# A transformer block on one core: causal runs with their masked key tiles between full ones, keys stored once and read in halves, and the last block's expert rows returned to tokens by products with ones

## The reference, cut to what matters

```python
x = layernorm(x + attention(x))            # causal, 16 heads of 8, rotary q and k
h = x + msa(layernorm(x) * ln1_w + ln1_b)  # 16 heads of 8, every key seen, no mask
h = h + moe(layernorm(h) * ln2_w + ln2_b)
out = layernorm(x + h)

def moe(x):                                # 8 experts, hidden size 512
    e = argmax(x @ gate_w + gate_b)        # one expert for each token, the first of equals
    return gelu(x @ w1[e]) @ w2[e]
```

## Time and profile before

| | us |
|---|---|
| median of three runs | 893.57 |
| the profiled execution | 894.7 |
| its span, first to last instruction | 893.0 |
| TensorE busy | 809.2 (91%) |
| ScalarE busy | 775.7 (87%) |
| VectorE busy | 328.5 (37%) |
| GpSimd busy | 228.5 (26%) |
| mean granted TensorE clock | 0.959 |
| exp, L922, 832 instructions | 736.0 busy |
| first scores start | 33.31 |
| last run's sums taken by VectorE (L1312) | 815.87 |

### The profile page before, as it was taken

How to read it: one execution, slowest core, us unless ns; L and a number is a source line. 1 busy time by engine, 2 the same in 40 slices (tenths; PEclk the granted TensorE clock), 3 DMA queues, 4 the chain that set the end, 5 groups by cost and what they waited for, 6 DMA issues and landing times.

```text
span 893.0 us, 24266 instructions
## 1 busy us (share of the span) xinstructions
PE 809.2 (91%) x9940; PEld 369.5 (41%) x9952; DVE 328.5 (37%) x948; ACT 775.7 (87%) x906; POOL 228.5 (26%) x367
## 2 busy tenths in 40 slices
PE   8689999999999998999999999999999999996271
PEld 4244444444443443444344444444444444443240
DVE  5434525312430014320042433255332363334763
ACT  3579889999999998999999999999999899994440
POOL 5542211111110010000003343323334141443382
PEclk9799999999999999999999999999999999998575
DMA  8977220202110431810201000301000010001001
GB/s 273 269 210 224 96 49 2 95 2 49 49 48 1 108 84 40 244 50 3 48 2 32 1 3 3 78 8 37 3 3 19 14 43 3 1 3 31 30 14 41
DMA packets 34644, 51.60 MB, mean 58 GB/s; under 512 B 4064, under 2 KB 15072, under 8 KB 34528
## 3 DMA queue, kind: packets, MB, share of 16 engines
q1 hardware_dynamic: 32992, 46.30, 18.2%
q0 software_dynamic: 1536, 3.67, 1.3%
HBM read 29.12 MB, written 20.84 MB: 56 GB/s over the span
## 4 chain that ended last, share of the span: by engine, by line
PE 76%; DVE 8%; ACT 4%; issue 4%; DMA 2%; SPq 2%; POOL 2%; POOLq 1%; another core or an unknown queue 1%; DVEq 0%; ACTq 0%
PE ps L488 72%; ACT probs L922 3%; PE ps L493 3%; PE ps L787 1%; POOLq L1070 1%; DMA query_rows<-q_scratch 1%; POOL parts L1077 1%; DVE ln_newton L1156 1%; DMA q_scratch<-parts 1%; DVE q_rotated L1312 1%; DVE ln_newton L1155 1%; DVE z_rows L1176 1%; DVE ln_stats L1161 0%; DVE ln_newton L1154 0%
## 5 line engine op out<-in xcount | busy, mean ns | idle before, releaser
L922 ACT ACTIVATE probs<-ps 128x1024 f32<-128x1024 f32 (+3 forms) x832 | 736.0, 1017 | 41.5 <-PE ps L488 35.1
L488 PE MATMUL ps<-probs,values 128*9 128x256 f32 (+1 forms) x6528 | 426.3, 374 | 4.7 <-DVE q_rotated L1312 3.1
L488 PE MATMUL ps<-query_rows,key_rows 32*128 32x512 f32 (+3 forms) x1664 | 282.5, 485 | 17.5 <-ACT probs L922 10.2
L488 PEld LDWEIGHTS ps<-probs,values 128*9 128x9 f32 x6528 | 143.3, 90 | 182.5 <-issue 94.4
L488 PEld LDWEIGHTS ps<-query_rows,key_rows 32*128 32x128 f32 x1664 | 117.3, 183 | 183.5 <-issue 93.1
L1043 POOL TENSOR_SCALAR_AFFINE_SELECT probs<-probs 128x256 f32<-128x256 f32 x128 | 53.0, 420 | 234.4 <-ACT probs L922 231.5
L1090 POOL COPY parts<-early_late 128x512 f32 x63 | 44.5, 744 | 124.6 <-PE ps L488 124.6
L1048 POOL DMA_INDIRECT z_sorted<-z_rows,slot_numbers x16 | 15.8, 988 | 218.3 <-DVE slot_numbers L1447 208.8
L1312 DVE COPY q_rotated<-ps 128x512 f32<-128x512 f32 x30 | 20.7, 690 | 124.7 <-PE ps L488 124.6
L1077 POOL COPY parts<-parts 128x512 f32 x72 | 44.9, 663 | 29.3 <-PE ps L488 28.8
L1324 DVE RECIPROCAL recip<-ps 128x16 f32<-128x16 f32 x32 | 8.2, 256 | 70.5 <-PE ps L493 65.1
(11 more groups left out here) (184 smaller groups left out, 586.4 us busy)
## 6 DMA issues: line engine op xcount, KB each, us to landing
k_scratch<-parts SPq DMA_DIRECT2D x16, 512.0 KB, 3.9
q_scratch<-parts SPq DMA_DIRECT2D x16, 512.0 KB, 5.5
query_rows<-q_scratch SPq DMA_DIRECT2D x32, 256.0 KB, 5.3
key_rows<-k_scratch SPq DMA_DIRECT2D x20, 256.0 KB, 4.6
key_rows<-k_scratch SPq DMA_DIRECT2D x16, 192.0 KB, 4.5
parts<-in_w SPq DMA_DIRECT2D x1, 2048.0 KB, 8.9
early_late<-in_w SPq DMA_DIRECT2D x8, 256.0 KB, 8.0
early_late<-z_sorted SPq DMA_DIRECT2D x4, 384.0 KB, 3.1
```

The lines of the kernel that those rows point to most:

```text
L488: return nc.tensor.matmul(out, l, r, start=start, stop=stop, skip_group_check=True)
L922: nc.scalar.activation(Pr[:, t % KEPT, 2 * p:2 * p + 2, lo:BLK], score_banks(t, p)[:, :, lo:BLK], ACT.Exp, bias=-SHIFT[r["a"]], scale=SCAL ...
```

## The change

Its parts, in the order of the program:

1. **Loads.** Weights, block mask and identity move from SP's queue to ScalarE's queue; VectorE rotates block 0 before it waits for the identity.
2. **Keys stored once.** `k_scratch` loses a dimension: a block of keys is written by one DMA of 512 KB in place of two, and read by eight DMAs of 16 partitions in place of four of 32 (the same bytes). Queries are as before.
3. **First rows.** Of block 0, group 0's key and query rows are read first, with semaphores of their own; the other groups' rows follow.
4. **Order of key tiles.** The masked tiles of a causal run are dealt between full ones.
5. **Inverse root.** One cubic step (four small operations) takes the place of two Newton steps (six) in the layer norm; the same in `rows_to_h`, where the last `due` becomes one step earlier than `z_turn`.
6. **Routing.** Two reductions and three operations on all four tiles take the place of `max`, `max_index` and the rest.
7. **Gathers** of blocks 0 and 1 are paced at steps 4, 6, 8 and 10.
8. **Last block.** `up` of round 2 stands before `turn` of round 0; `up` of round 0 waits for the first turned tile alone. The store and the four gathers go away: a row of slot numbers is made by a product with ones, VectorE makes for each round a 128 by 512 matrix of ones and zeros, and TensorE sums `ones` times results over the six rounds (`m_sum`, four products each) in one bank, which VectorE adds.

```diff
-RDMA = 16 * HG
+RDMA, KDMA = 16 * HG, 16 * HG * NP
+ORDER = (
+    (0, 1, 2, 3),
+    (0, 1, 2, 3, 6, 4, 7, 5),
+    (0, 1, 2, 3, 4, 5, 11, 6, 10, 7, 9, 8),
+    (0, 1, 2, 3, 4, 5, 6, 7, 8, 15, 9, 14, 10, 13, 11, 12),
+)
-AT_END = side_order(*(range(first, first + 6 * ROUNDS, 6) for first in (30, 38, 43)))
+AT_END, TAKEN_AT_END = (side_order((30, 36, third, 48, 54, 60), range(38, 74, 6), range(43, 79, 6)) for third in (37, 42))
 ...
         def keys_out(a, b):
             sp.wait_ge(A[a]["k_split"], b + 1)
-            for i in range(NP):
-                sp.dma_start(k_scratch[a - 1, i, ...], k3[:, b]).then_inc(k_out[b], 16)
+            sp.dma_start(k_scratch[a - 1, ...], k3[:, b]).then_inc(k_out[b], 16)
+        def key_rows_in(a, g0, g1, t0, t1, done):
+            src = k_scratch[a - 1].rearrange("j d (g f) t -> f (j d) g t", f=HG)
+            each = ROWS // NP
+            for n in range(HG * NP):
+                sp.dma_start(kaf[n * each:(n + 1) * each, g0:g1, t0:t1], src[n // NP, :, g0:g1, t0:t1]).then_inc(done, 16)
+        def first_rows():
+            sp.wait_ge(k_out[0], 16)
+            key_rows_in(1, 0, 1, 0, BLK, k_first)
+            sp.wait_ge(q_out[0], 32)
+            query_rows_in(1, 0, 0, 1, q_first)
+            key_rows_in(1, 1, G, 0, BLK, k_rows[0])
+            query_rows_in(1, 0, 1, G, q_rows[0])
+        def places_in():
+            sp.wait_ge(evac_done, len(RUNS))
+            sp.dma_start(given_places, places_d).then_inc(ld_n, 16)
 ...
         def keys_there(r):
+            if r["n"] == 0:
+                pe.wait_ge(k_first, KDMA)
+                pe.wait_ge(q_first, RDMA)
+                return
 ...
-                side_free(b, k, ("sorted", 1))
+                side_free(b, k, ("sorted", 4 * r * TS // BLK))
+        def m_dest_rows():
+            pe.wait_ge(m_diag, 1)
+            mm(ps[:, 0, :], onesf[:, :], att[...]).then_inc(m_row, 1)
+        def m_sum(r):
+            pe.wait_ge(m_taken, taken(b, "down", r))
+            pe.wait_ge(m_at, r + 1)
+            for i in range(TB):
+                last = mm(ps[:, 1, i * P:(i + 1) * P], ones_at[r].bitcast(F32)[:, i * P:(i + 1) * P], yS[:, r, :],
+                          r == i == 0, r == ROUNDS - 1)
+        m_dest_rows()
         for k, (_, name, r) in enumerate(AT_END):
+            if name == "down" and r:
+                m_sum(r - 1)
             side_op[name](b, k, r)
+        m_sum(ROUNDS - 1)
 ...
         # scalar queue: the loads of wa, blk, ident first; wo ... kc after the first Exp
+                if r >= 2:
+                    act.wait_ge(m_side, issued(b, "turn", r - 2))   # before xg[r % 2] is written
         # gpsimd
+                if b == NB - 1:
+                    return
-                        pace(first_step(2, b + 2) + 1 + i)
+                        pace(first_step(2, b + 2) + 4 + 2 * i)
         # vector
+            def root_start(y, h, c, var, v):
+                ts(c, var, CUBIC, CUBIC * EPS, ALU.mult, ALU.add)
+                ts(h, var, -0.5, -0.5 * EPS, ALU.mult, ALU.add)
+                link(ts(y.bitcast(I32), v.bitcast(I32), -0.5, 1597463007.0, ALU.mult, ALU.add))
+            def cubic(y, c, t, u):
+                link(tt(t, y, y, ALU.mult))
+                link(tt(t, t, c, ALU.mult))
+                link(stt(out=u, in0=t, scalar=-1.25 / CUBIC, in1=t, op0=ALU.add, op1=ALU.mult))
+                link(stt(out=y, in0=u, scalar=1.875, in1=y, op0=ALU.add, op1=ALU.mult))
-                rsqrt(y, v, h, t, 1)
+                root_start(y, h, c, mv[:, :, 1], v)
+                cubic(y, c, t, u)
                 between()
-                newton(y, h, t, 2)
+                newton(y, h, t, 1)
-                due(13)
+                due(PREP_AT[b][0] - 1)
 ...  # route
-                max, max_index, copy, four is_equal
+                link(nc.vector.tensor_reduce(mx, lg[:, :, :], AX.X, ALU.max))
+                link(tt(oh, lg, mx, ALU.is_equal))
+                link(tt(lg, oh, first_wins, ALU.mult))
+                link(nc.vector.tensor_reduce(mx, lg[:, :, :], AX.X, ALU.max))
+                link(tt(oh, lg, mx, ALU.is_equal))
+            def dest_diag():
+                for i in range(TB):
+                    ins = ts(att[:, i, :], ident[:, :], destf[:, i:i + 1], None, ALU.mult)
+                ins.then_inc(m_diag, 1)
+            def ones_of(r):
+                dve.wait_ge(ld_n, 16)
+                dve.wait_ge(m_row, 1)
+                ts(ones_at[r], ps[:, 0, :], place_of[:, r:r + 1], None, ALU.is_equal).then_inc(m_at, 1)
 ...  # end of the program on VectorE
             route(b)
+            dest_diag()
             add_experts(b - 1)
             finish(b - 1)
-            experts(b, AT_END, at_once)
-            for i in range(TB):
-                dve.wait_ge(m_tile[i], 16)
-                link(tt(row, row, yback[:, i, :], ALU.add))
-                last = nc.vector.bn_stats(st[:, i, :], row)
-            normalize(xb, xb).then_inc(m_out, 1)
+            experts(b, TAKEN_AT_END, at_once)      # ones_of(r) behind the gelu argument of round r
+            dve.wait_ge(m_summed, 1)
+            link(tt(xb, xb, ps[:, 1, :], ALU.add))
+            layernorm(xb, xb).then_inc(m_out, 1)
```

More of the change, by code:

```diff
@@ L38 @@
 THETA = 10000.0
+CUBIC = float(np.sqrt(3.0 / 8.0))
 P = 128
@@ L320, in build @@
             sem(n) for n in ("a2_z", "a2_zT", "a2_hT", "k_blockdiag_set", "low_mm", "low_taken"))
+        ld_n = sem("ld_places")
+        m_diag, m_row, m_at, m_summed = (sem(f"m_{n}") for n in ("dest_diag", "dest_rows", "ones_at", "y_summed"))
         m_z, m_zT, m_h, m_g, m_oh, m_rank, m_dest, m_owner = (
             sem(f"m_{n}") for n in ("z", "zT", "h", "g", "oh", "rank", "dest", "owner"))
-        m_tile = [sem(f"m_y_back_tile{i}") for i in range(TB)]
         m_w1_last = sem("m_w1_staged_last")
@@ L341, in build @@
         kaf, qaf = KAv.bitcast(F32), QAv.bitcast(F32)
+        ones_at = [(KAv[:, 3, r * BLK:(r + 1) * BLK] if r < 4 else KAv[:, r - 3, S - BLK:S]) for r in range(ROUNDS)]
+        given_places = Pr[:, KEPT - 1].rearrange("p h t -> p (h t)")[:, 0:SORTED + ROUNDS]
+        places, place_of = given_places[:, 0:SORTED], given_places[:, SORTED:SORTED + ROUNDS]
         values_of = {1: V, 2: V2}
@@ L349, in run_step @@
         def run_step(r, n):
-            causal, kt = r["a"] == 1, r["k0"] + n
+            causal = r["a"] == 1
+            order = ORDER[r["qb"]] if causal else range(r["k0"], r["k1"])
+            kt = order[n]
             cut = causal and kt >= r["qb"] * TB
-            done = sum(TB for q in RUNS[:r["n"]] if q["a"] == 1)
+            done = r["n"] * TB + sum(k >= r["qb"] * TB for k in order[:n])
             return dict(r=r, t=r["t0"] + n, kt=kt, lo=(kt % TB) * P if cut else 0,
-                        cut=2 * (done + kt % TB) + 1 if cut else None, start=n == 0, stop=kt == r["k1"] - 1)
+                        cut=2 * done + 1 if cut else None, start=n == 0, stop=n == len(order) - 1)
         block = ctx.enter_context(nc.Block())
@@ L402, in query_rows @@
                 sp.wait_ge(q_out[b], 32 * a)
[L403 to L409 removed]
+                query_rows_in(a, b, 0, G, q_rows[b % 2])
@@ L1118, in _ @@
                 for r in runs_in(1, qb):
-                    for i in range(TB):
-                        cut(run_step(r, qb * TB + i))
+                    for n, kt in enumerate(ORDER[qb]):
+                        if kt >= qb * TB:
+                            cut(run_step(r, n))
                     if r["n"] == 0:
@@ L1469, in experts @@
             def experts(b, order, due):
-                for k, (at, name, r) in enumerate(order):
+                for at, name, r in order:
+                    k = [op[1:] for op in (IN_SHADE if b < NB - 1 else AT_END)].index((name, r))
                     if name == "turn" and b < NB - 1:
@@ L1635 @@
             (p[:, None] // ROWS == np.arange(HG)[None, :]).astype(np.float32)], axis=1),
+        places=np.concatenate([np.tile(np.arange(SORTED), (P, 1)), p[:, None] + P * np.arange(ROUNDS)[None, :]],
+                              axis=1).astype(np.float32),
     )
```

136 lines of the change are left out of this document (68 added, 68 removed).

## The result

The changed kernel takes 884.77 us, the median of four runs (882.34 to 886.25); the kernel before took 893.31 beside it (892.58 to 898.55). The ratio is 0.9889, with a 95% interval of 0.9845 to 0.9934: faster by 1.1%, and 15 us slower than the forecast of 869.6. By the bounds that the prediction set (884.6 to 902.5 is no change), this is no change, to which it gave a chance of 0.04. The profiled execution took 886.25 us, its span 884.5.

A forecast was written before the change was run, and what follows sets the result against it. Three places were taken to bound the kernel: attention's start, exp spacing and the tail. 894.7 - 5.2 - 6.7 - 2.3 - 2.0 - 7.8 = 870.7, less 1.1 for the median, gave 869.6 us, range 860 to 880.

The forecast's parts named there:

- Step 1: Start: parts 1 to 3 bring first scores and the gating input rows earlier; -5.2 us, bounds 1 and 9.
- Step 2: Causal attention: dealing masked key tiles between full ones cuts ScalarE's starving, 0.65 us a run in blocks 2 and 3; -6.7 us.
- Step 3: Second attention's first query block: last Newton step before the evac removes TensorE's wait for z rows; -2.3 us.
- Step 4: Rest of the second attention: shorter layer norms give 1.2 us and spread gathers 0.8; -2.0 us.
- Step 5: Tail: routing and layer norms -2.0, `dest_diag` and `up` -0.3, rounds +1.5, store and gathers replaced -7.0; -7.8 us.
- A: Expert rounds: VectorE binds them, ScalarE and GpSimd wait on it, costing 6 us and more; 874.1 us, chance 0.16.
- B: Start: input rows don't gate because SP's stream ends earlier than thought; start -9, 865.8 us, chance 0.12.
- C: Causal runs: all of ScalarE's starving goes, -19 in place of -6.7; 857.3 us, chance 0.08.
- D: Start: ScalarE's 16 loads back up, its first copies come late, rows land no earlier; 873.8 us, chance 0.08.
- E: Causal runs: the new tile order gains nothing, the 1.6 us of starving only moves; 876.3 us, chance 0.06.
- F: Tail: `dest_diag` and block 2's layer norm wait out GpSimd's scatters and copies; 872.9 us, chance 0.06.
- G: Causal runs: every masked step becomes as slow as a full TensorE step with transposes, +26 us; 902 us, chance 0.03.

The follow-up runs named there:

- eight_by_groups: Changed kernel with keys written twice again and a block read by eight DMAs of 32 partitions and two head groups: 883.12 us, ratio 0.9843.
- keys_twice: Changed kernel with keys written twice again and a block read by four DMAs of 32 partitions: 877.55 us, ratio 0.9787.
- before_once: Kernel before with only part 2 made, keys written once and read by eight DMAs of 16 partitions: 902.18 us, ratio 1.0056.
- before_x: Kernel before with one DMA moved, the input rows issued right behind the query rows of block 1: 893.0 us, ratio 0.9994.
- due13: Changed kernel with input rows issued early, loads back on SP's queue, and due(13) again before the last Newton step: 875.69 us, ratio 0.9755.
- pace_old: Changed kernel with input rows issued early, loads back on SP's queue, and gathers again at steps 1 to 4: 876.5 us, ratio 0.9777.
- ones_once: Changed kernel with input rows early, loads back on SP's queue, ones matrix made for round 0 only (last block's output wrong): 872.05 us, ratio 0.9763.
- before_loads: Kernel before with only part 1 made, loads on ScalarE's queue and block 0 rotated before the identity wait: 897.01 us, ratio 1.0017.
- x_early_part: Changed kernel with input rows issued early and only the first group of loads back on SP's queue: 874.21 us, ratio 0.9794.

## Why the prediction was wrong, step by step

**Step 1, the start: -5.2 predicted, +9.2 measured.** The mechanism was right: what attention gains in front of the input rows is lost at their gate, and they stand at the end of SP's stream. The step that failed is the term for SP's stream: four key writes less, 5.3, while eight issues of 0.6 against four reads of 1.17 "cost almost nothing". It priced a read into 16 partitions by its bytes, half of 1.17 or less. The runs show that such reads go at 148 GB/s where those of 32 partitions go at 246, with the DMA engines full in both. For 1 MB that is 7.1 against 4.3: 2.8 more a block, against 1.3 for the write left out. The issuing was not free either: eight DMAs for four, bytes and partitions alike, made the rows 3.4 late (eight_by_groups against keys_twice). So the one part that was to shorten SP's stream made it longer, and alone it makes the kernel before slower (before_once). The input rows came 6.5 us later, not 4.4 earlier. Of these, 3.5 are the new reads alone; 2.9 come only where block 0's rows are split as well, which the prediction had put at 0.9 of gaps. Why the two together cost more than each is not shown by an experiment of its own; the trace shows SP issuing block 0's reads until 30.59, in place of 26.21.

The lower bound was too narrow as well. No row of before showed a read into 16 partitions; the nearest row from below is that each takes as long as one of 32, 1.17. That gives 8 x 1.17 = 9.4 for 4.7, and the late rows would have been inside. I had bounded only the issuing, and that wrongly: 16 extra issues of 0.6 are 9.6, so a bound for which they aren't hidden is a loss of about 4, not a gain of 1. The rule quoted from the Trainium skill, DMA: Bandwidth & Descriptors, section Rules for kernel authors (transfers to disjoint partition halves serialize), speaks against the halves, and the measured rate agrees with its direction; it is not enough for the size, since reads that only queue up would have taken the old 4.7.

A late row costs more than its lateness. Five kernels give a line (start of VectorE's sum against the start of run (1,1), and that run's length):

| | sum starts | run starts | late by | run (1,1) |
|---|---|---|---|---|
| before | 77.82 | 77.99 | -0.2 | 14.93 |
| keys_twice | 76.29 | 72.82 | 3.5 | 19.85 |
| before_once | 80.80 | 77.59 | 3.2 | 20.41 |
| eight_by_groups | 81.22 | 74.33 | 6.9 | 23.75 |
| after | 84.29 | 74.38 | 9.9 | 26.91 |

Against 14.5 (14.9 with the old order), each loss is 1.8 to 2.5 more than the lateness: behind the stall TensorE's granted clock is down, 0.59 of full from 88.5 to 94 us in the changed kernel, and full from 94 on. It also means that starting attention earlier than the rows allow brought nothing.

"Without the wait for the identity VectorE starts some 2 us earlier" failed too. VectorE's first rotation waits for TensorE's product, which ends at about the same time: 9.34 after 7.36 of waiting for TensorE, and 8.06 with the loads on SP's queue, for 8.23 before. And the loads on two queues brought the first product to 5.45 from 4.34. TensorE was ready for scores at 30.64, not at 27 to 28.8; first scores at 26 to 29 us with no half clock after them, named as a sign, did not come: they start at 30.64, and the granted clock was 0.50 to 0.52 from 34 to 42 us.

**Step 2, the order: -6.7 predicted, -4.7 measured**, of which 1.14 in the first run of query block 2 is a stretch of lower clock (0.73 granted from 125 to 130 us) that only the profile before has; before_x, with the same order, takes 21.13 there for 22.27. So the order itself gave about 3.5, half of what was predicted. Clean runs gained 0.52 to 0.61 for 0.65, a 16-step one takes 27.3, just over the 27.2 named as a sign. The mis-sized part is the runs where side work goes on: the first run of query block 2 gained 0.07, the second lost 0.55, the second of block 3 gained 0. That side work and masked steps meet there is the likely reason; no run tests it. **Step 3: -2.3 predicted, -2.4 measured**; due13 brings the wait back and so shows its cause. **Step 4: -2.0 predicted, -3.0 measured.** The layer norm gave 0.44 to 0.57 in each of three query blocks, as worked out; the gathers' spreading gave 2.2 and was put at 0.8, and pace_old gives 2.4 back; 0.6 is lost again in other runs. Since before_x shows no stall with the old pacing, part of the 2.2 is the luck of the profile before.

**Step 5, the tail: -7.8 predicted, -7.6 measured**, part by part: routing takes 1.65 (829.39 to 831.04) for 2.73 (830.67 to 833.40), 1.1 less for 1.2; the rounds, from the first gelu argument to the last result, 24.97 (850.12 to 875.09) for 23.70 (852.31 to 876.01), so 1.3 lost for 1.5; from the end of the last result to the aggregate 878.33 - 875.38 = 2.95 for the predicted 3.1.

**The rivals.** A is ruled out by ones_once: the added VectorE operations of five rounds are worth 0.7. B had the input rows not gating, the opposite of what happened. C did not occur, E neither. D was half right: the loads' move gained no time by itself, but not because ScalarE's queue backed up. F: one VectorE operation took 3.92 beside GpSimd's copies, but from the statistics to the normalized rows it took 8.11 (836.85 to 844.96) for 8.16 before, so nothing was added. G's loss in the masked steps did not occur. The case that occurred, a slower transfer in front of a known gate, was none of the rivals, though the gate was named.

## What to carry to other kernels

A DMA that is split by partitions is not half as long (here 0.93 us for a half against 1.17 for the whole): price it at the whole duration until a row shows less, and count its issues, above all when it stands in a queue ahead of something waited for. When a wait is found near a gate, move what is waited for ahead in its queue first: one moved DMA gave 10 us of the changed kernel's time, and nothing in the kernel before, where the gate was just met. Then look at what else the change makes earlier, because all of it ends at the first gate that has not moved.

## What the runs showed of the hardware beside that

- Key reads with 2 KB rows: into 16 partitions, each source row fetched twice from one copy, 147 and 148 GB/s in two kernels; into 32 partitions 244 (the kernel before, 53 to 58 us) and 246; all with the DMA engines busy 1.00 or more.
- After a TensorE wait of 2.35 us for z the run behind it was 1.5 to 1.6 longer still in three of five profiles (due13, before_once, before_loads), with a granted clock of 0.79 in the 8 us behind the wait, and not in before, where it was 1.00, and before_x.
- With masked tiles last, four of five profiles lose 1.1 to 1.2 us in one run of query blocks 2 and 3 (granted clock 0.66 to 0.76 in the mean of 5 us of it); with the tiles dealt out, none of twelve does.
- TensorE's first eight products took 5.1 to 6.8 us in profiles of kernels with the same products: each takes 0.85 us at first and 0.43 later, and the change comes after three to seven of them. The profile's rows don't show it: in the kernel before they have a granted clock of 1.00 from 4.4 to 8 us, where products take 0.85, as from 8 to 10. The one profile left out is x_early_part, with its wait among them.
